# Row-maximum products over 64 rows a head, the two heads of a pair side by side in TensorE's order

## What is computed

```python
q = _rope(q, theta); k = _rope(k, theta)
scores = jnp.einsum('bhqd,bhkd->bhqk', q, k) * scale
scores = jnp.where(causal, scores, -jnp.inf)
attn = jax.nn.softmax(scores, axis=-1)
ctx = jnp.einsum('bhqk,bhkd->bhqd', attn, v)
```

## Time and profile before

| | |
|---|---|
| Median of 3 executions | 2695.24 us (2693.89 to 2697.93) |
| The profiled execution | 2697.22 us |
| Its span, first to last instruction | 2695.4 us |
| Mean granted TensorE clock | 0.914 |
| TensorE busy (products) | 2221.6 us |
| VectorE busy | 2126.0 us |
| ScalarE busy | 1097.0 us |
| GpSimd busy | 1071.1 us |
| Row-maximum products, L1464 | 768 in 320.5 us |
| Their reductions, L1087 and L1090 | 512 in 245.8 us, 256 in 176.0 us |

### The profile page before, as it was taken

The page is one execution under the profiler, slowest core; times in us unless marked ns, Lnnn a source line. Parts: engine busy times, 40 slices in busy tenths (PEclk is TensorE's granted clock), DMA queues, the critical chain, the costliest instruction groups (busy, mean ns, idle before and its releaser), DMA issues.

```text
span 2695.4 us, 45060 instructions
## 1 busy us (share of the span) xinstructions
PE 2221.6 (82%) x11094; PEld 1323.7 (49%) x11094; DVE 2126.0 (79%) x3845; ACT 1097.0 (41%) x1825; POOL 1071.1 (40%) x994
## 2 busy tenths in 40 slices
PE   3659999879765999987966699998796569999789
PEld 1235565547423555554732456554572245555466
DVE  4968888769496888876949688886795878888678
ACT  3314343337521434344742144443474123434266
POOL 2035555433103646543310465554330054646332
PEclk9879999879796999987979699999797979999889
DMA  1000000001000000000100000000110000000011
GB/s 57 0 24 5 5 8 4 0 20 41 11 0 24 5 9 4 4 1 24 39 9 0 24 5 9 4 4 1 32 31 9 7 18 9 5 8 0 9 30 33
DMA packets 36370, 35.78 MB, mean 13 GB/s; under 512 B 4008, under 2 KB 31120, under 8 KB 36240
## 3 DMA queue, kind: packets, MB, share of 16 engines
q1 hardware_dynamic: 36240, 34.27, 4.3%
HBM read 32.16 MB, written 2.10 MB: 13 GB/s over the span
## 4 chain that ended last, share of the span: by engine, by line
PE 56%; DVE 19%; issue 13%; ACT 7%; POOL 3%; DVEq 2%; ACTq 1%; DMA 0%; POOLq 0%; SPq 0%
PE ps L1450 8%; PE ps L1464 6%; PE ps L1235 5%; PE ps L1432 5%; PE ps L1236 5%; PE ps L1237 5%; PE ps L1434 4%; PE ps L1351 3%; DVE state L962 3%; DVE ps L1087 3%; DVE cs L970 3%; PE ps L1506 2%; ACT q_split L738 2%; PE ps L1263 2%; DVE inverse L1020 2%
## 5 line engine op out<-in xcount | busy, mean ns | idle before, releaser
L755 ACT ACTIVATE probs<-ps 128x512 f32<-128x512 f32 (+3 forms) x768 | 352.2, 488 | 492.4 <-PE ps L1437 258.5
L1464 PE MATMUL ps<-k_high,q_split 128*128 128x512 f32 (+3 forms) x768 | 320.5, 433 | 63.4 <-POOL k_high L485 35.0
L604 POOL TENSOR_TENSOR prob_sums<-prob_sums,probs 128x512 f32<-128x512 f32 (+3 forms) x256 | 237.4, 927 | 309.7 <-ACT probs L755 298.3
L1432 PE MATMUL ps<-q_split,k_high 128*128 128x512 f32 (+3 forms) x768 | 307.4, 401 | 21.7 <-ACT probs L755 15.5
L1450 PE MATMUL ps<-probs,vals 128*64 128x512 f32 (+3 forms) x1536 | 325.3, 509 | 0.0
L1464 PEld LDWEIGHTS ps<-k_high,q_split 128*128 128x128 f32 x768 | 155.3, 204 | 251.1 <-issue 113.5
L1087 DVE CUSTOM_DVE_ANT_0 ps<-ps,row_masks 128x128 f32<-128x128 f32 (+3 forms) x512 | 245.8, 499 | 34.5 <-PE ps L1464 33.6
L1434 PE MATMUL ps<-q_max,k_low 65*128 65x512 f32 (+7 forms) x768 | 269.5, 351 | 0.0
L566 POOL TENSOR_TENSOR roped<-turned 128x1024 f32<-128x1024 f32 x64 | 155.5, 2429 | 240.6 <-DVE turned L1061 227.8
L1193 DVE TENSOR_TENSOR hg_low<-hg,hg_high 128x512 fp32r<-128x512 f32 x256 | 231.1, 903 | 0.7 <-ACT hg_high L793 0.7
L730 ACT ACTIVATE q_max<-ps 1x512 fp32r<-1x512 f32 x128 | 75.2, 588 | 378.6 <-PE ps L1351 377.8
(11 more groups left out here) (231 smaller groups left out, 5014.1 us busy)
## 6 DMA issues: line engine op xcount, KB each, us to landing
w<-in_w SPq DMA_DIRECT2D x128, 128.0 KB, 2.1
w_pair<-in_w_pairs SPq DMA_DIRECT2D x36, 256.0 KB, 2.6
xin<-in_x SPq DMA_DIRECT2D x5, 512.0 KB, 3.9
out<-acc SPq DMA_DIRECT2D x4, 512.0 KB, 3.7
pos<-in_c_pos SPq DMA_DIRECT2D x1, 512.0 KB, 4.9
v_w<-in_v_w SPq DMA_DIRECT2D x1, 512.0 KB
o_w<-in_o_w SPq DMA_DIRECT2D x1, 512.0 KB
v_b<-in_v_b SPq DMA_DIRECT2D x1, 512.0 KB
```

The source lines that it names most:

```text
L604: pool.tensor_tensor(total, before, probs[:, u % RING, 1, at:HALF], ALU.add).then_inc(p_added, 1)
L755: act.activation(probs[:, u % RING, h, q0 - HALF * c:HALF], ps[:, 4 + h, 0:w], ACT.Exp, scale=SCALE).then_inc(blocks_taken, 1)
L1432: pe.matmul(o, k_high[1 - par][h][:, j * P:(j + 1) * P], q_split[1 - par][h][:, q0:q0 + w], start=True, stop=False)
L1464: pe.matmul(o, q_split[par][h][:, i * P:(i + 1) * P], k_high[par][h][:, k0:k0 + w], start=True, stop=True).then_inc(scores_out, 1)
```

## The change

The "mx" items of a unit now stand side by side, head 0 and head 1. In each u from 4 to 11 there is one such pair, between the two "st"; in u = 6 and 9 a second one follows behind "pv"; the last two pairs follow behind the "pv" of u = 12 and u = 13. Head 0 contracts over rows 0 to 63 (upper part of q with upper part of k), head 1 over rows 64 to 127 (the same parts, q from `q_max`). The row maxima are thus taken from the product of the upper parts alone. Banks and semaphore counts follow the new order: product number 2u + h.

```diff
@@ slots(do_prev, do_this)
-    mx = [("mx", h, u) for h in range(2) for u in range(NU)]
+    mx = list(range(NU))
     out = []
     for u in range(NU + PV_LAG):
-        def rows():
-            return [mx.pop(0)] if do_this and u >= MX_FROM and mx else []
+        def rows(at_u=True):
+            if not (do_this and u >= MX_FROM and at_u and mx):
+                return []
+            i = mx.pop(0)
+            return [("mx", 0, i), ("mx", 1, i)]
 
         if do_prev and u < NU:
             out.append(("st", 0, u))
             out += rows()
             out.append(("st", 1, u))
-        out += rows()
         if do_prev and u >= PV_LAG:
             out.append(("pv", 0, u - PV_LAG))
-        out += rows()
+        out += rows(u in ROWS_TWICE or u >= NU or not do_prev)
...
-    return out + (mx if do_this else [])
+    return out + ([("mx", h, i) for i in mx for h in range(2)] if do_this else [])
...
 MX_FROM = 4
+ROWS_TWICE = (6, 9)
...
@@ VectorE
-                            dve.wait_ge(scores_out, 2 * NU * n + NU * h + u + 1)
-                            scores = ps[:, MX_BANK[u % 3], 0:w]
+                            dve.wait_ge(scores_out, 2 * NU * n + 2 * u + h + 1)
+                            scores = ps[:, MX_BANK[(2 * u + h) % 3], 0:w]
...
-                                dve.wait_ge(scores_taken, 2 * NU * n + NU * h + NU + 3)
+                                dve.wait_ge(scores_taken, 2 * NU * n + 2 * u + h + 1 + 3)
...
@@ TensorE
-                            if u == 0:
+                            if u == 0 and h == 0:
...
-                            pe.wait_ge(scores_taken, 2 * NU * n + NU * h + u + 1)
-                            o = ps[:, MX_BANK[u % 3], 0:w]
-                            pe.matmul(o, q_split[par][h][:, i * P:(i + 1) * P], k_high[par][h][:, k0:k0 + w],
+                            pe.wait_ge(scores_taken, 2 * NU * n + 2 * u + h + 1)
+                            o = ps[:, MX_BANK[(2 * u + h) % 3], 0:w]
+                            q_of = (q_split, q_max)[h][par][h]
+                            own = slice(HD * h, HD * h + HD)
+                            pe.matmul(o, q_of[own, i * P:(i + 1) * P], k_high[par][h][own, k0:k0 + w],
                                       start=True, stop=True).then_inc(scores_out, 1)
```

## The result

The changed kernel takes 2784.54 us (median of 4 executions, 2783.48 to 2786.25), the kernel before 2696.28 us in the same comparison. The ratio is 1.0329, with a 95% interval from 1.0311 to 1.0347: 88 us slower. The forecast was 2759, its range 2710 to 2796.

The account below looks back on a forecast made before the run. VectorE bounds from a step's last quarter to 5 us into the next, elsewhere TensorE. -0.1 and 2.4 make 2.3 us a step, times 28 is 64 us: 2761, less 2.0 for the median, 2759 us; range 2710 to 2796.

Parts of the forecast that it names:

- The switch: TensorE going to 64 rows and again going back: 0.19 us each time, bounds 0 and 0.20.
- Running together: A unit's two 64-row head products share TensorE's array; bounds 0 and 1.92 us saved per step.
- rival (a): The two heads' products don't run together on TensorE: 3.4 us more a step, 2790 us; chance 0.15.
- the wait that tears the third pair: Up to u = 9, the third pair's second product waits for a VectorE reduction: 0.82 us shrinks to about 0.5.
- VectorE's queue costs 2.4 us per step: From u = 10 on, VectorE's reductions, sum and maxima delay the next step's second "turned" from 8.55 to 11.0 us.
- the marks on the way: From u = 10: output products 4.38, eleventh unit's products 6.05, VectorE's start on them 6.59, second projection 9.9 us.
- The last step of each batch: Counted among the 28 steps, so priced at the same 2.3 us loss as every other.
- The wait at the second projection: In the next step TensorE waits over 1 us there for the last of the 24 reductions.
- Rival (b): Slack at the step's end hides VectorE's queue, leaving TensorE's own sum: 0.9 us a step, 2720 us; chance 0.10.
- this part is -0.1: Step up to u = 9: TensorE's net +0.20 us, less a shortened wait, gives -0.1 us a step.
- VectorE's busy time stays: Sign that the forecast is right: VectorE's busy time is unchanged, 39.0 us in the profiled steady step.
- (c): Going from 128 to 64 rows is no switch on TensorE: -0.4 us a step, 2684 us; chance 0.12.

Follow-up runs that it names:

- experiment 2: Kernel before, its order kept, but each row-maximum product contracts over its head's 64 rows: 2810.94 us, ratio 1.0420.
- experiment 11: Changed kernel with both heads in rows 0 to 63, so nothing runs together, and GpSimd's probability sums cut to 8 columns behind each half's first: 2800.04 us.
- experiment 1: Changed kernel with its new order kept, but each product contracts over all 128 rows again: 2758.49 us, ratio 1.0227.
- experiment 7: Changed kernel reordered: 64 rows only for pairs right behind the probability products, 128 rows for five units, no pair behind the step's end: 2758.06 us.
- experiment 6: Changed kernel with 128 rows in every product and second pairs in u = 6 to 9, so none stands behind the step's end: 2727.53 us.
- experiment 5: Changed kernel with product banks in another turn; the next step's second to fourth projections each wait only for their own bank's reduction: 2786.21 us.

## Why the forecast came out as it did

**The switch.** 0.19 us for each change between 128 and 64 rows, read from 8-row products at the start of the trace, was right to the hundredth (experiment 2's rows). The load that comes only with its product was read from the same rows. In the changed kernel it is there at each of the 340 changes to 64 rows and the 340 back. The Trainium skill, TensorE: Matmul & The Clock Gate, Part 2, lets a load be pulled ahead of running products if their rows don't conflict with it or if it goes to a background buffer; across a change of rows the trace of the changed kernel never shows it.

**Running together.** Right in the mechanism: where no reduction is missing the starts are 0.00 to 0.01 us apart, and experiment 11 gives the 1.5 us a step that rival (a) put on the columns. Rival (a) is out. The forecast had foreseen the wait that tears the third pair, but not those of the eighth and the last.

**The end.** "VectorE's queue costs 2.4 us per step" was the largest term and right in place and nearly in size (2.74 as the mean of all 28 steps): the marks on the way came out at 4.50, 6.18, 6.70 and 9.96 us where the forecast had 4.38, 6.05, 6.59 and 9.9. Measured on the whole end it is 2.6 us in one half of the steps (15.23 from 287.00 to 302.23, against 12.64) and 2.9 in the other. The half with 2.9 is the one in which VectorE's program comes to the edge of its loop: 0.64 us pass before "turned", 0.20 in the other. That term was missing. The last step of each batch, which the forecast priced like the others, lost only 1.6 (13.15 against 11.57); this makes up for part of it, by luck. The wait at the second projection, forecast at over 1 us, is 0.79 at the loop's edge and 1.1 inside it. Before the change the two halves differ by 0.03 us only (12.64 and 12.67): nothing was late at the edge. Rival (b), slack that hides the queue, is out: experiment 1 shows the 2.65 us with no switch in it.

**The front.** The forecast was -0.1 us, measured +0.25 in the step of the table and +0.12 as the mean of all 28. The step that failed is "this part is -0.1", and under it the forecast that VectorE's busy time stays. The reductions did cost what they did before; it is VectorE's sums that slide onto GpSimd's. With GpSimd's sums cut on both sides the front is 30.92 against 31.18, -0.26; so the collisions that came with the order account for what the forecast lacked, and a little more.

**The clock.** The granted clock fell once a batch at a second projection, in three batches that of the loop's last step and in one that of the step before it. I had not forecast it. The changed kernel around that place (columns as in the earlier trace rows):

```profile
484.00:486.50 2.50, 2.19 (x11) 0.98 (x9) 2.40 (x8) 0.00 (x0) 0.06 (x1) 1.00 0.00 0
486.50:490.00 3.50, 2.70 (x12) 1.15 (x12) 2.48 (x6) 0.00 (x0) 0.00 (x0) 0.61 0.00 0
```

The stretch ahead is at 1.00; the one with the second projection, which starts at 487.30 after a wait of 1.11 us, has a mean of 0.61. The end there takes 16.69 us and not 15.23, so this costs about 1.5 us in three batches and 1.1 in the fourth, 5.5 in all. Before the change no step of the loop shows it. What decides when it falls stays open: waits just as long, in the other steps of the same kind, left the clock at 1.00.

**The sum.** Over the 28 steps the forecast had -3 us for the front and +67 for the end; the traces show +3.4 and +76.6, 5.5 of it the clock. With the 6 us outside these steps, for which the forecast had nothing, that is the gap between its 64 us and the 86 between the two spans (88 between the medians). Cause, place and order of size were right. The sum was too small because three small terms, each a delay that lands where nothing covers it, all go the same way.

**The rival of the other side.** (c) needed a change of rows to cost under 0.03 us. It costs 0.19. Its remark that the end's queue would still be there holds: experiment 1 has no changes between 128 and 64 rows and is 60 us slower.

## What to carry to other kernels

Packing two half-height products side by side saves the columns of one, here 0.21 us for 512 columns; getting into that mode and out of it costs 0.38. By these prices it could pay only where several pairs follow each other, or where the mode changes anyway; this is an estimate, and experiment 7, the one try at it, did not show a gain. Whoever reorders products for one engine should list what the other engine then has to do behind the last of them: here that list, not the mode, made two thirds of the loss. And look at which instructions of VectorE and GpSimd now run at the same time.

No version of the new arrangement beat the kernel before; the nearest, experiment 6, is 31 us slower.

## What the runs showed of the hardware

- A VectorE sum with both inputs in SBUF that starts while GpSimd runs a sum of its own nearly always ends only after it: 1.69 us instead of 0.69 for 512 columns, and in the changed kernel 56 of 59 such sums end 0.55 us after GpSimd's. The profile counts the delay as busy time. So a busy time that grows with the same work is a sign to look for.
- The clock of TensorE fell to the 1.2 GHz level behind 12 of the 24 waits of 1.7 to 1.9 us in experiment 5. In the changed kernel it fell behind three waits of 1.11 us and one of 0.80, and stayed at 1.00 behind the others of the same lengths. These runs show the cost, 0.9 to 1.5 us each time, but not what decides.
- At the edge of its loop VectorE stood idle for 0.64 us before "turned", at the same place inside the loop for 0.20. Before the change the ends of the two kinds of step differ by 0.03 us only.
